# Three PSUM copies of a gated linear-attention kernel move from VectorE to ScalarE

## The reference, cut to what matters

```python
xn = _layernorm(x, axis=-1)
# attention branch: 16 heads of 64, L2-normed q and k, decaying causal weights
q = _l2norm((x @ Wq)...); k = _l2norm((x @ Wk)...); v = x @ Wv
dt = softplus(x @ Wa + dt_bias); alpha = exp(-exp(A_log) * dt)
cum_log = cumsum(log(alpha + 1e-08))
l_mat = where(causal, exp(cum_log_i - cum_log_j), 0)
out = ((q @ k^T) * l_mat) @ v
out = out * rsqrt(mean(out * out) + 1e-06) * rms_w
attn = out * silu(x @ Wg) @ Wo
# feed-forward branch: activations quantised to 8 bits, weights to -1, 0, 1
h = gelu(bitlinear(x, w1, b1)); ffn = bitlinear(h, w2, b2)
x = x + attn(xn) + ffn(xn)
```

## Time and profile before

| | us |
|---|---|
| device time, median of 2 runs | 6266.1 (6246.54 and 6285.65) |
| the profiled execution, its own time | 6217.22 |
| its span on the slowest core (core 2) | 6215.7 |
| spans of the 8 cores | 6189.4 to 6215.7 |
| busy on that core: PE, PE weight loads, DVE, ACT | 3203.1, 1758.9, 1917.3, 1217.0 |

### The profile page before, as it was taken

One profiled execution on the slowest core, in us unless ns is written; L12 is line 12 of the kernel. 1 busy time (PEld: TensorE's weight loads), 2 busy tenths in 40 slices (PEclk: granted clock), 3 DMA queues, 4 the chain that ended last, 5 costly groups with the idle time before them and its releaser, 6 DMA issues.

```text
span 6215.7 us, 54756 instructions; the slowest of 8 cores (6189.4 to 6215.7 us)
## 1 busy us (share of the span) xinstructions
PE 3203.1 (52%) x17994; PEld 1758.9 (28%) x17994; DVE 1917.3 (31%) x3835; ACT 1217.0 (20%) x2490; POOL 155.2 (2%) x278
## 2 busy tenths in 40 slices
PE   0255556445454555554453425555555555555555
PEld 0133344333333333332332312222222222222222
DVE  1343443343434343333333312222222222222222
ACT  0111111111111111111111112222222222222222
POOL 0000000000000000000000000000000000000000
PEclk9865655555656565655555658888888888888888
DMA  3110110111101010101101140000000000000000
GB/s 100 56 45 26 46 43 27 56 34 39 51 30 46 27 45 25 46 26 54 34 30 49 36 136 24 24 24 24 24 24 24 24 24 24 24 24 24 24 21 20
DMA packets 109196, 230.68 MB, mean 37 GB/s; under 512 B 53845, under 2 KB 54630, under 8 KB 103798
## 3 DMA queue, kind: packets, MB, share of 16 engines
q1 hardware_dynamic: 91702, 180.74, 9.6%
q0 software_dynamic: 17216, 46.45, 2.1%
HBM read 155.54 MB, written 58.72 MB: 34 GB/s over the span
## 4 chain that ended last, share of the span: by engine, by line
PE 36%; DVE 25%; issue 13%; ACT 10%; DMA 9%; SPq 6%; DVEq 1%; ACTq 0%; POOL 0%; POOLq 0%
PE PY L1012 8%; PE PSM L700 6%; SPq L878 4%; PE PVG L545 3%; DVE BPART L913 3%; ACT HG L908 3%; PE PYW L948 3%; DMA scr_w2q<-WQP 2%; PE PH L897 2%; PE PSM L704 2%; SPq L146 2%; DVE PBF L719 2%; PE PK L743 2%; PE PK L504 1%; PE PVG L728 1%
## 5 line engine op out<-in xcount | busy, mean ns | idle before, releaser
L897 PE MATMUL PH<-W1Q,XQF 128*128 128x512 bf16 x2048 | 539.3, 411 | 654.2 <-DMA XQF<-scr_xq 520.1
L1012 PE MATMUL PY<-W2Q,HQF 128*128 128x512 bf16 x2048 | 484.5, 379 | 140.4 <-DVE HQF L1004 121.3
L897 PEld LDWEIGHTS PH<-W1Q,XQF 128*128 128x128 bf16 x2048 | 192.2, 102 | 947.7 <-issue 790.4
L913 DVE TENSOR_REDUCE BPART<-HG 128x1 f32<-128x512 f32 x256 | 175.6, 686 | 915.7 <-ACT HG L908 915.7
L700 PE MATMUL PSM<-UFLAT,ONE 1*128 1x128 f32 x1024 | 405.6, 497 | 0.0
L719 DVE TENSOR_TENSOR PBF<-PQS,EBF 128x128 bf16<-128x128 f32 x512 | 136.0, 291 | 866.5 <-ACT EBF L711 864.8
L545 PE MATMUL PVG<-WG,XNF 128*128 128x512 bf16 x512 | 184.9, 541 | 395.6 <-DVE VB L540 395.6
L711 ACT ACTIVATE EBF<-PSM,WNT 128x128 bf16<-128x128 f32 x512 | 146.3, 367 | 1191.6 <-PE PSM L704 1191.5
L1012 PEld LDWEIGHTS PY<-W2Q,HQF 128*128 128x128 bf16 x2048 | 182.1, 97 | 401.8 <-issue 220.3
L481 PE MATMUL PSM<-WAB,XNF 128*128 128x16 bf16 x256 | 11.6, 174 | 547.4 <-DVE XNF L478 547.4
L988 ACT ACTIVATE HQI<-HG,c_qs 128x512 int8<-128x512 f32 x256 | 184.7, 722 | 477.0 <-DVE HQS L994 446.7
(11 more groups left out here) (206 smaller groups left out, 4720.3 us busy)
## 6 DMA issues: line engine op xcount, KB each, us to landing
WST<-w1t SPq DMA_DIRECT2D x32, 1024.0 KB, 5.9
WST<-w2t SPq DMA_DIRECT2D x64, 512.0 KB, 3.8
XCH<-x SPq DMA_DIRECT2D x32, 512.0 KB, 6.2
XRES<-x SPq DMA_DIRECT2D x32, 512.0 KB, 6.2
y<-GT SPq DMA_DIRECT2D x32, 512.0 KB, 3.0
scr_xq<-XQB POOLq DMA_DIRECT2D x32, 256.0 KB, 2.3
scr_g<-GB POOLq DMA_DIRECT2D x32, 256.0 KB, 2.3
scr_att<-ATB POOLq DMA_DIRECT2D x32, 256.0 KB, 3.3
```

The source lines that it names most:

```text
L897: fns = [(lambda os=os, kt=kt, pp=pp: lambda e: e.matmul((PH1 if pp == 0 else PH2)[:, 0:512], XQF[:, kt * 128:(kt + 1) * 128], W1Q[:, kt * ...
L913: one("v", (lambda os=os: lambda e: e.reduce_max(out=BPART[:, os:os + 1], in_=HG[:, os * 512:(os + 1) * 512], axis=AX, apply_absolute_valu ...
L1012: lambda e: e.matmul(PY[:, ns * 512:(ns + 1) * 512], HQF[pp][:, i * 128:(i + 1) * 128], W2Q[:, kt * E + ns * 512: kt * E + (ns + 1) * 512] ...
```

## The change

Three copies out of PSUM, all in `phaseA_chunk`, are put in ACT's stream instead of DVE's. They stand at the same places of the source, with the same operands. The rounding to bf16 of XNF and the float32 of EUW stay.

```diff
-        one("v", lambda e: e.tensor_copy(out=XNF[:], in_=PQS[:]),
+        one("s", lambda e: e.copy(out=XNF[:], in_=PQS[:]),
             reads=[rPQS], writes=[rb["XNF"]])
...
-        one("v", lambda e: e.tensor_copy(out=EUW[:], in_=PVG[:]),
+        one("s", lambda e: e.copy(out=EUW[:], in_=PVG[:]),
             reads=[rPVG], writes=[rb["EUW"]])
         one("v", lambda e: e.tensor_mul(QTF[:], PQS[:], EUW[:]),
...
-        one("v", lambda e: e.tensor_copy(out=EUW[:], in_=PVG[:]),
+        one("s", lambda e: e.copy(out=EUW[:], in_=PVG[:]),
             reads=[rPVG, rb["EUW"]], writes=[rb["EUW"]])
         one("v", lambda e: e.tensor_mul(KHF[:], PK[:], EUW[:]),
```

## The result

The changed kernel takes 6297.8 us in the median of 11 runs, the kernel before 6220.3 in the median of 10. The ratio is 1.0122, its 95% interval 1.0091 to 1.0153. That is 77.5 us or 1.2% slower: clear of noise, and by the 2% of the verdict "same". The level of before had been known from two runs only (6266.1); the median of all ten lies 46 us lower, next to the profiled execution.

What follows compares the result with a forecast made beforehand. No engine is full, so the chain of hand-overs, with KB's start, bounds the kernel. The terms 116 - 23 - 13 - 1 - 11 = +68 us on the 6266.1 us median give 6334 us, range 6285 to 6395.

Steps and rivals of the forecast that it cites:

- Term A: Chunks 1 to 8 and 17 to 24, XNF behind weight sums on ACT: KB 7.26 us later each, +116 us.
- Term B: Chunks 9 to 16: XNF on ACT starts ahead of DVE's clipping passes, 2.9 us a chunk gained, -23 us.
- term C: Chunks 25 to 31: XNF ahead of shorter clipping passes, 1.9 us a chunk gained, -13 us.
- Chunk 0's -1: Chunk 0 has its transposes ready about 1.1 us before DVE is free: -1 us.
- The copy: 128x1024 copy from PSUM on ACT: 1.05 us, bounds 0.85 to 1.37, against 1.22 to 1.23 on DVE.
- Term D: The two EUW copies, with their hand-overs, are faster on ACT: -0.33 us a chunk, -11 us over 32 chunks.
- The 0.05 for a slower hand-over: In the EUW copies' estimate, some 0.05 us allowed for a slower hand-over from PE to ACT.
- Fully hidden: Rival: ACT's lateness covers XNF's new place behind the weight sums entirely, that cost is 0, time 6218; chance 0.06.
- nothing hidden: Rival: KB not held by L494, XNF's whole delay behind weight sums counts, 180 us, time 6398; chance 0.06.
- Table loads: Rival: ACT's XNF and EUW copies need another function table, 164 us of loads, time 6498; chance 0.04.
- A slow copy: Rival: the ACT copy takes 1.37 us or a little above, +31, time 6365; at 1.6 us 6387; chance 0.05.
- The signs: What would show the forecast: copy time, PE's XNF wait, L494 and KB waits, XNF spacing, L642 to L666, phase B unchanged.

Runs made afterwards that it cites:

- e4: Kernel before, all copies on DVE, with the weight sums of chunks 0 to 7 and 16 to 23 moved inside the chunk: 6149.0 us, ratio 0.9891.
- e1: Kernel before with only XNF moved to ACT, EUW copies left on DVE: 6313.5 us against 6215.7, ratio 1.0157.
- e2: Kernel before with only the two EUW copies moved to ACT: 6198.5 us, ratio 0.9974.

## Why the prediction was right

The forecast was +68 us or 1.1%, and +77.5 or 1.2% came out. The step on which it rests, that XNF's delay is paid only so far as it passes what L494 paid before, is what e4 and the lags of KB show. The measured time lies in the stated range, 6285 to 6395. Two errors partly cancel in it: the level of before was 46 us too high, since two runs had to stand for it, and the difference 10 us too low. So 6334 was 36 us too high.

**Term A, +116.** Measured +119.8 (60.0 and 59.8). The reasoning, that a KB already held by ACT through L494 pays 7.26 us more whether ACT is late by 9 or by 14, is what the two equal numbers show, and e4 shows the held part by itself. The missing 4 us have two parts. From the end of the sums' last record on ACT to KB it was 0.60 us before and is 7.98 now, mean of the 16 chunks and eight cores: 7.38 more and not 7.26. In it the K matmuls, taken at 5.70 us, were 6.00, while the copy (0.99, taken at 1.05) and the step from its end to the first K matmul (0.98, taken at 1.09) were shorter. And ACT came free 0.11 us later a chunk than before, which the prediction had put at nothing.

**Term B, -23, and term C, -13.** Measured -25.9 and -15.8. XNF starts 2.83 and 1.88 us sooner after ATB, close to the 2.75 and 1.77 of the terms. But from its start to KB it takes 0.41 and 0.38 us less, not 0.17. The copy is 0.23 shorter, and the first K matmul follows its end by 0.10 us less. Chunk 0's -1 came out: from the end of its transposes to KB it takes 8.39 us and not 9.38.

**The copy, 1.05 us (0.85 to 1.37).** Measured 992 ns for XNF and 1012 ns for EUW. The estimate from the Trainium skill, "VectorE: DVE Perf Modes", section on the TRN2 errata, was 1.00 us and was the better one. The way over the two instructions that read PSUM gave 1.11, and 1.02 with the 0.09 off, which is within 3%. Rounding that up to 1.05 made it 4 to 6% high.

**Term D, -11.** The step is right and the sum is seen only beside the right kernel. In the changed kernel the stretch from L642 to L666 shrank by 0.44 us a chunk, mean of the eight cores, so 14 us in all, but the body of the chunks lost just 0.8 against before. The kernel to compare with is e1, which has XNF on ACT and the EUW copies on DVE: its body is 2700.4 us, and the two EUW copies take it to 2686.8, 13.6 less (9.8 on cores 0 to 3, 17.5 on cores 4 to 7). In e2, without XNF on ACT, they gave 11.7. So what ate the term isn't the EUW copies but XNF, which lengthened the body by 12.8 in e1, and for which the prediction had no term. The 0.05 for a slower hand-over from PE to ACT, which is in the -0.33, isn't seen: EUW starts 0.10 us after the end of L642 on ACT, against 0.12 on DVE.

Where XNF costs in the body is partly to be named: at the G matmuls. The groups of before and of after (busy us, mean ns, idle before):

```profile
L545 PE MATMUL PVG<-WG,XNF 128*128 128x512 bf16 x512 | 184.9, 541 | 395.6 <-DVE VB L540 395.6
```
```profile
L545 PE MATMUL PVG<-WG,XNF 128*128 128x512 bf16 x512 | 189.6, 551 | 319.0 <-DVE VB L540 319.0
```

Same instructions, 4.7 us more. Taken by groups of chunks, it goes with the granted clock. The table has cores 4 to 7, whose clock has half and full speed alone in both kernels. The clock is the mean share of full speed over the stretch in which the G matmuls of a chunk run; 0.617 says that it stood at full for about a quarter of it.

| chunks | G matmuls before, us a chunk | clock | after | clock |
|---|---|---|---|---|
| 1-8 | 5.84 | 0.617 | 6.14 | 0.582 |
| 9-16 | 5.91 | 0.607 | 5.87 | 0.611 |
| 17-24 | 5.63 | 0.643 | 6.06 | 0.590 |
| 25-31 | 5.49 | 0.671 | 5.44 | 0.677 |

The matmuls got slower where the clock in their stretch fell, and nowhere else. These are the chunks in which XNF now stands behind the weight sums. In e1 the G matmuls take 6.6 us more than before, mean of the cores. There they got slower in all four groups, and the clock of each fell, by 0.013 to 0.053. The rest of the lengthening, some 6 of e1's 12.8 us, is spread over the chunk, and no run here tells what it hangs on.

**The rivals.** "Fully hidden" and "nothing hidden" are both out: 7.5 us a chunk appeared, neither 0 nor 8.4 and 14.1. "Table loads" is out, XNF starts at 346.41 with nothing between it and the sum ahead, and no core has a table load between the first XNF and the end of phase A. The prediction's reading that before has them in phase B alone passed over one at 188 us, ahead of the first chunk, which stands in both kernels. "A slow copy" is out at 1.0 us.

**The signs.** PE's wait for XNF was to rise to about 700 us and rose to 703.2. KB was to wait for the K matmuls in all 32 chunks and does. From one XNF to the next it takes 7.8 and 8.6 us more where the weight sums stand, and 3.6 less where the scaling stands, where about 7 and 2 to 3 were named. From L642 to L666 it is 0.44 shorter, where 0.3 was named. Chunks 17 to 24 lengthened no more than chunks 1 to 8, measured from ATB to KB, and what follows the last ATB, phase B in the main, is 1.1 us of 2592 longer. One sign can't be seen as it was put: L494 was no longer to wait for an ACT held by the weight sums, but its wait rose, from 204.8 to 247.9 us, because what it needs comes from an XNF that itself stands behind the sums. It no longer holds KB, and that is what counts.

## What to carry to other kernels

Before an instruction is moved to an idle engine, look at what stands directly ahead of it in that engine's stream, and what that waits for. An engine at 20% busy can still be late each time it is needed, if its work waits for loads: here one and the same copy cost 7.5 us a chunk behind two or four load-bound sums, and gained 1.35 us with these moved out of the way. And a delay that is seen in a wait (156 us here) isn't the loss: follow the chain to the next instruction that was late anyway, and price only the difference.

Side work with long waits, as the weight sums and the scaling here, is better placed inside the loop body, where its engine idles, than between two bodies, where every engine's next work stands behind it. That order was worth 6.4% with all copies left on DVE, far more than which engine makes a copy.

## What the runs showed of the hardware that I had not expected

- ACT copies 128x1024 float32 from PSUM in 992 ns to bf16 and in 1012 ns to float32, as a CAST or a COPY and with no table load, against 1218 and 1225 ns on DVE (medians of the slowest core, kernels after and before).
- A hand-over from ACT to DVE or back takes 0.09 to 0.10 us from the end of one to the start of the next. Two dependent instructions on DVE itself, EUW and QTF, lie 0.10 us apart too. Alternating ACT and DVE on one buffer costs nothing extra between the two. Behind it PE takes up L728 0.11 us later in all five kernels with the EUW copies on ACT, a cost whose cause is open.
- The K and the G matmuls got slower by 3% each (179.4 to 184.2 us and 183.4 to 188.2, mean of cores 4 to 7) when XNF moved, though nothing about them changed. In chunks 1 to 8 the K matmuls went from 5.47 to 6.06 us as the mean granted clock over them went from 0.674 to 0.597. Matmul durations in this kernel aren't constants to be carried from one order to another: they go with the granted clock of their stretch.
